# A perceiver block on one core: the order of the first loads and products, and of the last 32 microseconds

## The chip, the cores and the metric

The kernel runs on one core of a Trainium2 chip. The core has TensorE (PE, matmuls; its weight loads are the rows PEld), VectorE (DVE), ScalarE (ACT), GpSimd (POOL) and SyncE (SP, which here only issues DMAs), each with an instruction stream of its own; they wait for each other on semaphores. The metric is device time of one execution in microseconds, as the median of several runs; a lower time is better. TensorE's clock has two levels, 1.2 and 2.4 GHz; a profile gives the granted share (0.50 or 1.00).

## What is computed

Three residual layers over x, 8 x 64 tokens of 1024 numbers, all in float32, cut here to what matters:

```python
x = x + xattn(layernorm(x), ctx_4096, ...)     # cross attention, 32 heads of 128, 8 kv heads
x = x + attn(layernorm(x), Wq, Wk, Wv, Wo)     # causal self attention, 32 heads of 32
x = x + ffn(layernorm(x), W_res, W_pre, W_post, bases, gate, W_branch)

def ffn(x):                                     # 4 streams of 256 for each token
    x_norm = x * rsqrt(mean(x * x) + eps)
    logits = x_norm @ [W_res; W_pre; W_post].T + base          # 24 numbers a token
    H_res  = sinkhorn_log(logits[:16].reshape(4, 4))           # 50 iterations of row and column sums
    H_pre, H_post = softmax(logits[16:20]), softmax(logits[20:24])
    H_res  = (1 - g) * I + g * H_res
    y      = einsum('nc,n->c', streams, H_pre) @ W_branch
    return einsum('ij,jc->ic', H_res, streams) + outer(H_post, y)
```

## The kernel before

The 512 tokens are four tiles of 128 rows, t = 0 to 3; `xr[:, t, :]` is tile t of x in SBUF. A weight is used in units of 512 x 1024: a unit is loaded into `raw`, transposed there by DVE in four pieces (`turn_first`, `turn_unit`; two of the eight column chunks a piece), and split into a high part (`hi_w`, ACT, semaphore `w_hi`) and a low part (`lo_unit`, a subtraction on DVE, semaphore `w_lo`). Activations are split in the same way (`hi_ln` on ACT, `ln_lo_half` on DVE). A product takes three matmuls for each of 8 chunks c: p = 0 is high times high, p = 1 uses the low part of the weights, p = 2 the low part of the activations. The order on every engine is the order of the code; there is no scheduler.

**The start.** SP and ACT issue the loads of x and of unit 0. Unit 0 comes in two halves of 1 MB (`first_unit(0)`, `first_unit(1)`, four DMAs of 256 KB each, two from SP and two from ACT). The code numbers chunks so that a half of the columns gives chunks 0 to 3 and the other chunks 4 to 7. DVE takes the statistics of a tile (`first_stats`), POOL its power of -0.5 (`ln_root`, `ln_move`), ACT normalises into `hb`, PE transposes it (`turn_ln`), and ACT and DVE split the result. PE starts the products of unit 0 (`products`, from `query_unit(0, ...)`), for tile 0 by chunks: `chunks=True` makes it wait for `w_lo` of each chunk. The transposes of the next tile are put between the products of the present one (`between`, at the product `at`, 11 if nothing is given).

**The end.** The last 16 groups of 24 products are b = 0 to 15 (`tile_products`, with hooks `at_5`, `at_11`, `at_17` after products 5, 11 and 17). Around them PE transposes finished tiles (`turn_rows`) and multiplies them by the 24 columns of the ffn's logits (`logits`, 8 small matmuls a tile). Group b = 15 gives the last half of tile 3; DVE adds it (`add_last(3, 1)`), PE transposes it and finishes the logits of tile 3, and only then can the second of two Sinkhorn chains start on DVE. Chain 0 holds tiles 0 and 1, chain 1 tiles 2 and 3; each operation of a chain is on 128 x 32 or 128 x 8 numbers and waits for the one before it (`stepped`, semaphores `sk_step`). Chain 0 is 12 iterations ahead (`LEAD`); the rest of its iterations alternate operation by operation with those of chain 1, and the last 11 iterations of chain 1 run alone. When a chain is done, ACT writes 16 diagonal matrices a tile (`diagonals`) and PE uses each for a matmul of 256 columns (`mix`); ACT copies the result (`mixed`) and SP stores it. Tile 3 is mixed on DVE instead. In the wait for the chains PE does `branch` and `base`.

## Time and profile before

| | |
|---|---|
| median of 3 runs | 1115.98 us (1114.47 to 1116.58) |
| profiled execution, its own time | 1116.33 us |
| profiled execution, span of the core | 1114.5 us |
| busy in the span | PE 1066.1, PEld 895.4, DVE 815.9, ACT 479.1, POOL 190.8 us |
| moved | 111.26 MB |

The span runs from the first to the last instruction; the 1.8 us that the execution's own time has beside it lie around the program. Starts in rows below are microseconds from the start of the span.

### The profile page before, as it was taken

To read this page: it belongs to the slowest core of one execution; us is meant where nothing else is said; L and a number is where in the kernel's file an instruction comes from. 1 tells how busy PE (TensorE), PEld (TensorE's weight loads), DVE (VectorE), ACT (ScalarE), POOL (GpSimd) and SP (SyncE) were. 2 spreads that over 40 slices of the span, in tenths; PEclk is the share of its full clock that TensorE was granted. 3 is DMA by queue.
4 is the path that set the end of the run, shared out by engine and by line. 5 is a ranking of instruction groups with operands and counts; after the bars stand their busy time and mean duration, and the time that the engine had idled before them with its cause. 6 is when DMAs were issued, how large, how long until landed. Compare 5 with 4: busy or idle time off the path is not lost.

```text
span 1114.5 us, 17571 instructions
## 1 busy us (share of the span) xinstructions
PE 1066.1 (96%) x6326; PEld 895.4 (80%) x6326; DVE 815.9 (73%) x1854; ACT 479.1 (43%) x1021; POOL 190.8 (17%) x186
## 2 busy tenths in 40 slices
PE   5999999999999999999999999999999999999638
PEld 3888888788888888888888888888888878887537
DVE  6787667676667879766668877666627788847997
ACT  4553444344445446544444465423213344431416
POOL 0000000233233232333233230000001032320000
PEclk9999999999999999999999999999999999998779
DMA  9785676245544333344444312799935423000001
GB/s 238 153 201 129 156 158 158 50 109 109 113 96 88 75 76 72 68 96 98 109 98 108 76 38 52 159 219 244 204 67 103 76 41 58 3 14 1 1 1 76
DMA packets 184540, 111.26 MB, mean 100 GB/s; under 512 B 108040, under 2 KB 174344, under 8 KB 184480
## 3 DMA queue, kind: packets, MB, share of 16 engines
q1 hardware_dynamic: 182224, 109.37, 45.3%
q10 hardware_dynamic: 2256, 1.11, 0.5%
q8 instruction: 35, 0.57, 0.2%
q14 instruction: 25, 0.20, 0.1%
HBM read 90.98 MB, written 18.94 MB: 99 GB/s over the span
## 4 chain that ended last, share of the span: by engine, by line
PE 91%; DVE 7%; DMA 1%; ACT 1%; issue 0%; ACTq 0%; POOL 0%; DVEq 0%
PE ps L608 32%; PE ps L515 15%; PE ps L575 14%; PE ps L943 9%; PE ps L501 4%; PE ps L636 4%; PE ps L619 4%; PE ps L932 2%; PE ps L719 1%; DMA raw<-in_L_xattn_q_proj_w 1%; DVE small L2057 1%; DVE small L2061 1%; DVE small L2049 1%; PE ps L852 1%; DVE small L2053 1%; DVE small L2045 1%
## 5 line engine op out<-in xcount | busy, mean ns | idle before, releaser
L608 PE MATMUL ps<-wt,act 128*128 128x512 f32 x1536 | 381.0, 394 | 0.0
L608 PEld LDWEIGHTS ps<-wt,act 128*128 128x128 f32 x1536 | 278.0, 188 | 51.8 <-issue 0.4
L515 PE MATMUL ps<-wt,act 128*128 128x512 f32 x768 | 178.0, 393 | 4.0 <-DVE wt L1513 4.0
L515 PEld LDWEIGHTS ps<-wt,act 128*128 128x128 f32 x768 | 145.2, 190 | 34.7 <-DVE act L1497 4.4
L575 PE MATMUL ps<-act,wt 128*128 128x512 f32 x672 | 153.7, 390 | 0.0
L1068 ACT ACTIVATE wt<-raw 128x512 fp32r<-128x512 f32 x192 | 106.3, 625 | 94.4 <-PE ps L515 52.6
L575 PEld LDWEIGHTS ps<-act,wt 128*128 128x128 f32 x672 | 125.8, 188 | 26.0
L1505 DVE STREAM_TRANSPOSE raw<-raw 128x1024 f32<-128x1024 f32 x92 | 107.9, 1216 | 21.4 <-DMA raw<-in_L_xattn_o_proj_w 21.4
L1513 DVE TENSOR_TENSOR wt<-raw,wt 128x512 fp32r<-128x512 f32 x176 | 109.9, 682 | 17.4 <-ACT wt L1068 17.4
L943 PE MATMUL ps<-wt,act 128*128 128x512 f32 x480 | 122.1, 402 | 0.0
L2209 POOL TENSOR_TENSOR small<-small 128x4 f32<-128x4 f32 (+2 forms) x64 | 69.0, 1080 | 257.9 <-DVE small L1527 211.5
L1170 ACT ACTIVATE G<-G,small 128x256 f32<-128x256 f32 x128 | 64.0, 502 | 102.1 <-DVE small L1641 102.0
L1497 DVE TENSOR_TENSOR act<-ps,act 128x512 fp32r<-128x512 f32 x80 | 53.9, 680 | 67.7 <-ACT act L1063 67.7
L943 PEld LDWEIGHTS ps<-wt,act 128*128 128x128 f32 x480 | 87.3, 189 | 17.6 <-POOL wt L2268 0.2
L2236 POOL TENSOR_TENSOR act<-xr,act 128x1024 fp32r<-128x1024 f32 x30 | 72.1, 2403 | 115.9 <-ACT act L1101 115.9
L1063 ACT ACTIVATE act<-ps 128x512 fp32r<-128x512 f32 x80 | 46.9, 596 | 82.8 <-PE ps L501 82.8
L501 PE MATMUL ps<-ident,G 128*128 128x128 f32 x448 | 66.9, 275 | 9.8 <-ACT G L1074 9.7
L2227 POOL TENSOR_TENSOR small<-small 128x4 f32<-128x4 f32 x32 | 12.2, 380 | 374.4 <-DVE small L1658 374.4
L501 PEld LDWEIGHTS ps<-ident,G 128*128 128x128 f32 x448 | 54.9, 141 | 22.1 <-issue 9.2
L619 PE MATMUL ps<-act 128*128 128x256 f32 x384 | 60.0, 291 | 0.6 <-issue 0.6
L1637 DVE SCALAR_TENSOR_TENSOR G<-ps,small,G 128x256 f32<-128x256 f32 x128 | 55.4, 474 | 5.1 <-PE ps L619 5.1
L636 PEld LDWEIGHTS ps<-act 128*128 128x128 f32 x384 | 54.3, 189 | 5.6 <-issue 0.4
(164 smaller groups left out, 1242.2 us busy)
## 6 DMA issues: line engine op xcount, KB each, us to landing
xr<-in_ctx SPq DMA_DIRECT2D x64, 256.0 KB, 4.8
raw<-in_L_xattn_o_proj_w SPq DMA_DIRECT2D x32, 512.0 KB, 14.1
raw<-in_L_xattn_q_proj_w SPq DMA_DIRECT2D x28, 512.0 KB, 8.9
xr<-q_rows SPq DMA_DIRECT2D x16, 512.0 KB, 4.2
ot_hi<-spare SPq DMA_DIRECT2D x64, 128.0 KB, 2.0
act<-ot_hi SPq DMA_DIRECT2D x32, 256.0 KB, 9.0
q_rows<-G SPq DMA_DIRECT2D x28, 256.0 KB, 2.6
raw<-in_L_xattn_k_proj_w SPq DMA_DIRECT2D x8, 512.0 KB, 7.2
```

What stands on the lines that cost most here:

```text
L501: tr = pe.transpose(bank[par][:, j * P:(j + 1) * P], src, ident[:])
L515: mm = pe.matmul(banks[t], lhs(p == 2, c, t), wt[:, n_slot, int(p == 1), c, :], start=(acc_from and q == 0), stop=(acc_to and q == 3 * NC ...
L575: mm = pe.matmul(acc[h], wt[:, par, int(p == 1), c, h * P:(h + 1) * P], act[:, 0, int(p == 2), c * UW:(c + 1) * UW], start=(q == 0), stop= ...
L608: mm = pe.matmul(bank, src[int(p == 2)][:, c, kt * P:(kt + 1) * P], wt[:, slot, int(p == 1), c, :], start=(q == 0), stop=(q == 3 * NC - 1))
L619: mm = pe.matmul(sacc[:, j * 256:(j + 1) * 256], lhs[p], kT[r][:, g, :], start=(p == 0 and r == 0), stop=(p == 1))
L636: mm = pe.matmul(oacc, vN[r][:, kt, g * P:(g + 1) * P], pT[p][:, kt * 256:(kt + 1) * 256], start=(n == 0), stop=(n == 5))
L943: mm = pe.matmul(acc2[t], act[:, int(n >= 23), int(p == 2), k:k + P], wt[:, n % 2, int(p == 1), c, :], start=(q == 0), stop=(q == 3 * NC - 1))
L1068: sc.activation(blocks16(wt_dst(par, 0, c)), raw_chunks(par, c) if slot is None else raw_chunks(slot, c), ACT.Copy).then_inc(w_hi, 1)
L1505: v.transpose(y, y).then_inc(w_turned, 1)
L1513: v.tensor_tensor(blocks16(wt_dst(par, 1, c)), raw_chunks(slot, c), blocks16(wt_dst(par, 0, c)).bitcast(F32), ALU.subtract).then_inc(w_lo, 1)
L2209: pool.tensor_tensor(dst, src, mhalf[:, 0:n], ALU.pow).then_inc(signals, 1)
L2236: pool.tensor_tensor(ctx_dst(ctxT, 1, kt), ctx_src(kt), ctx_dst(ctxT, 0, kt).bitcast(F32), ALU.subtract).then_inc(ctx_lo, 1)
```

## The change

- SP waits for tile 0 of x to have landed before it issues the load of tile 1, and everything behind it in its queue; ACT waits for the same before its two DMAs of the second half of unit 0.
- In unit 0, tile 0, PE no longer goes chunk by chunk: for chunks 0 to 3 first all p = 0, then p = 2, then p = 1, and then the same for chunks 4 to 7 (`by_half`). Tiles 1 to 3 take p = 2 last (`low_last`). Waits are now on `w_hi`, `hi_done`, `lo_done` and `w_lo` each where its operand is used. The transposes of tile 1 stand after product 15 instead of 11.
- The first four low parts of the weights move from DVE to POOL (`lo_first`). DVE takes the statistics of tile 1 right behind the first two transposes. ACT alternates between high parts of weights and of the activations.
- In group b = 15 the first half of tile 3's logits stands after product 5, not after product 17 behind tile 2's.
- The last 11 iterations of chain 1 are done as two interleaved chains of one tile each (names 1 and 2, 16 columns an operation).
- Before `mix(0)` PE waits until chain 0 is 30 operations from its end and does four matmuls with an identity into an unused bank. The wait ahead of `mix(1)` is gone.
- The last half of tile 2 is mixed, copied and stored in two quarters, from banks of their own.

```diff
@@ SyncE
             for dst, rows in first_unit(0)[0:2]:
                 sp.dma_start(dst, rows).then_inc(first_half, 16)
+            sp.wait_ge(x_loaded[0], 16)
             sp.dma_start(xr[:, 1, :], x_rows[:, 1, :]).then_inc(x_loaded[1], 16)
...
-            for t, half, signal, count in ((0, None, mix_out, 2), (1, None, mix_out, 4), (2, 0, mix_out, 5),
-                                           (3, 0, out_ready, 1), (3, 1, out_ready, 2), (2, 1, mix_out, 6)):
+            for t, i0, i1, signal, count in ((0, 0, 4, mix_out, 2), (1, 0, 4, mix_out, 4), (2, 0, 2, mix_out, 5),
+                                             (2, 2, 3, mix_out, 6), (3, 0, 2, out_ready, 1), (3, 2, 4, out_ready, 2),
+                                             (2, 3, 4, mix_out, 7)):
@@ TensorE
-                        c, p = divmod(q, 3)
+                        c, p = order[min(t, 1)][q] if order else divmod(q, 3)
                         if arrived and p == 0:
                             arrived(t, c)
-                        if chunks and t == 0 and p == 0:
+                        if order and p == 2 and c % 4 == 0:
+                            pe.wait_ge(lo_done, 2 * t + c // 4 + 1)
+                        if chunks and t == 0 and p == int(bool(order)):
                             pe.wait_ge(w_lo, NC * n + c + 1)
...
             def ln_ready(t, c):
+                if t == 0:
+                    pe.wait_ge(w_hi, c + 1)
                 if c % 4 == 0:
-                    pe.wait_ge(lo_done, 2 * t + c // 4 + 1)
+                    pe.wait_ge(hi_done, 2 * t + c // 4 + 1)
+            by_half = [(4 * g + j, p) for g in range(2) for p in (0, 2, 1) for j in range(4)]
+            low_last = [(c, p) for c in range(NC) for p in (0, 1)] + [(c, 2) for c in range(NC)]
-            query_unit(0, 0, lambda t: None, next_ln, chunks=True, arrived=ln_ready, at={1: 17, 2: 17})
+            query_unit(0, 0, lambda t: None, next_ln, chunks=True, arrived=ln_ready, at={0: 15, 1: 17, 2: 17},
+                       order=(by_half, low_last))
...
                     if b == 12:
                         logits(1)
+                    elif b == 15:
+                        logits(3, 0, 4)
...
                     if b == 15:
                         logits(2)
-                        logits(3, 0, 4)
...
+            pe.wait_ge(base_added, 3)
+            pe.wait_ge(sk_step[0], CHAIN_STEPS - 30)
+            for _ in range(4):
+                pe.matmul(ps[:, 6, :], ident[:], z[:, 0, 0:UW], start=True, stop=True)
             mix(0)
-            pe.wait_ge(sk_step[1], CHAIN_STEPS - 42)
             mix(1)
-            pe.wait_ge(mix_out, 1)
-            pe.matmul(mix_banks[2][1], ident[:], xr[:, 2, UW:E], start=True, stop=False)
+            pe.wait_ge(mix_out, 2)
+            for i in (2, 3):
+                pe.matmul(mix_bank(2, i), ident[:], xr[:, 2, i * CW:(i + 1) * CW], start=True, stop=False)
             mix(2)
@@ ScalarE
+            sc.wait_ge(x_loaded[0], 16)
             for dst, rows in first_unit(1)[2:4]:
                 sc.dma_start(dst, rows).then_inc(raw_loaded[0], 16)
             normalise(0)
-            hi_ln(0, 0, T)
-            for c in range(4):
-                hi_w(0, 0, c)
+            hi_w(0, 0, 0)
+            hi(0, 0, ln_dst(0, 0, 0), bank=T)
+            hi_w(0, 0, 1)
+            hi_w(0, 0, 2)
+            hi(1, 1, ln_dst(0, 0, 1), bank=T)
+            hi_w(0, 0, 3)
             normalise(1)
...
-            mixed(2, 1)
+            mixed_quarter(2)
+            mixed_quarter(3)
@@ VectorE
             turn_first(1)
+            first_stats(1)
             ln_lo_half(0, 0)
-            for c in range(4):
-                lo_unit(0, c)
-            first_stats(1)
             turn_first(2)
             turn_first(3)
             ln_lo_half(0, 1)
+            v.wait_ge(w_lo, 4)
             for c in range(4, NC):
                 lo_unit(0, c)
...
+            tiles[1:] = [(2, 1), (3, 1)]
+            ua[1:] = [uv[:, 8:12], uv[:, 12:16]]
+            ub[1:] = [uv[:, 24:28], uv[:, 28:32]]
+            iterated.append(iterated[1])
+            stepped(1)
             for _ in range(ITERS - iterated[1]):
-                iterate((1,))
-            finish_cols(1)
-            finish_gate(1)
-            finish_diagonal(1)
+                iterate((1, 2))
+            for c in (1, 2):
+                finish_cols(c)
+            for c in (1, 2):
+                finish_gate(c)
+            for c in (1, 2):
+                finish_diagonal(c)
@@ GpSimd
+            def lo_first(c):
+                pool.wait_ge(w_hi, c + 1)
+                pool.tensor_tensor(blocks16(wt_dst(0, 1, c)), raw_chunks(0, c), blocks16(wt_dst(0, 0, c)).bitcast(F32),
+                                   ALU.subtract).then_inc(w_lo, 1)
+            ln_root(0)
+            ln_move(0)
+            lo_first(0)
+            lo_first(1)
+            ln_root(1)
+            ln_move(1)
+            lo_first(2)
+            lo_first(3)
```

The first place is DVE at the start of the program. `BN_STATS` to `TENSOR_SCALAR` are a tile's statistics, `STREAM_TRANSPOSE raw` the turned weights (two rows a half), `act` rows the low part of the activations and `wt` rows the low parts of the weights. Before, from the transposes of the first half on:

```order
L1549 STREAM_TRANSPOSE raw<-raw 128x16x64 [waits first_half]
L1549 STREAM_TRANSPOSE raw<-raw 128x16x64
L1497 TENSOR_TENSOR act<-ps,act 128x4x128 [waits hi_done]
L1513 TENSOR_TENSOR wt<-raw,wt 128x512 [waits w_hi] x4
L1522 BN_STATS small<-xr 128x6 [waits x_loaded1]
L1522 BN_STATS small<-xr 128x6
L1524 BN_AGGR small<-small 128x2 [waits dv]
L1526 TENSOR_SCALAR small<-small 128x1 [waits dv]
L1527 TENSOR_SCALAR small<-small 128x1
L1549 STREAM_TRANSPOSE raw<-raw 128x16x64 [waits raw_loaded0]
```

And in the changed kernel:

```order
L1578 STREAM_TRANSPOSE raw<-raw 128x16x64 [waits first_half]
L1578 STREAM_TRANSPOSE raw<-raw 128x16x64
L1551 BN_STATS small<-xr 128x6 [waits x_loaded1]
L1551 BN_STATS small<-xr 128x6
L1553 BN_AGGR small<-small 128x2 [waits dv]
L1555 TENSOR_SCALAR small<-small 128x1 [waits dv]
L1556 TENSOR_SCALAR small<-small 128x1
L1526 TENSOR_TENSOR act<-ps,act 128x4x128 [waits hi_done]
L1578 STREAM_TRANSPOSE raw<-raw 128x16x64 [waits raw_loaded0]
L1578 STREAM_TRANSPOSE raw<-raw 128x16x64
L1526 TENSOR_TENSOR act<-ps,act 128x4x128 [waits hi_done]
L1542 TENSOR_TENSOR wt<-raw,wt 128x512 [waits w_hi,w_lo]
```

The statistics of tile 1 have moved ahead of the first `act` row, the four `wt` rows of chunks 0 to 3 are gone from DVE, and nothing but two short pieces now stands between the first transposes and the wait for the second half (`raw_loaded0`).

The second place is PE in group b = 15. `wt,act` rows are products, `ident,xr` rows transposes of a finished tile and `G,raw` rows of 128x24 logits. Before:

```order
L943 MATMUL ps<-wt,act 128x512 x24
L874 MATMUL ps<-ident,xr 128x128 x4
L943 MATMUL ps<-wt,act 128x512 x6
L883 MATMUL ps<-G,raw 128x24 x12
L943 MATMUL ps<-wt,act 128x512 x6
L874 MATMUL ps<-ident,xr 128x128 x4
L883 MATMUL ps<-G,raw 128x24 x4
```

And in the changed kernel:

```order
L958 MATMUL ps<-wt,act 128x512 x18
L899 MATMUL ps<-G,raw 128x24 x4
L958 MATMUL ps<-wt,act 128x512 x6
L890 MATMUL ps<-ident,xr 128x128 x4
L958 MATMUL ps<-wt,act 128x512 x6
L899 MATMUL ps<-G,raw 128x24 x8
L958 MATMUL ps<-wt,act 128x512 x6
L890 MATMUL ps<-ident,xr 128x128 x4
L899 MATMUL ps<-G,raw 128x24 x4
```

Of the 12 small matmuls that stood in one piece, 4 stand 12 products earlier; the last 6 products are behind the same work as before.

## Rows read from the trace of the kernel before

**Rows 1.** Page, 40 equal slices of the span: busy tenths of TensorE.

```profile
PE   5999999999999999999999999999999999999638
```

**Rows 2.** Busy time summed over the windows 43 to 500 and 500 to 984.

```profile
sum 941.00, PE 938.62 PEld 790.88 DVE 681.55 ACT 415.38 POOL 182.37; mean PE 469.31 PEld 395.44 DVE 340.78 ACT 207.69 POOL 91.19
```

**Rows 3.** Timeline of the start: start, duration, engine, instructions, [idle before, releaser].

```profile
11.46 2.37 DVE L1549 STREAM_TRANSPOSE raw<-raw 128x1024 f32<-128x1024 f32 x2 [4.65 <-DMA raw<-in_L_xattn_q_proj_w]
...
15.15 5.09 PE L515 MATMUL ps<-wt,act 128*128 128x512 f32 x12 [4.01 <-DVE wt L1513]
...
22.09 7.06 PE L515 MATMUL ps<-wt,act 128*128 128x512 f32 x30
...
43.04 7.42 PE L575 MATMUL ps<-act,wt 128*128 128x512 f32 x32
```

**Rows 4.** ACT's DMAs of the first half: issue time min/median/max, starts; then issue to landing.

```profile
L1083 ACTq DMA_DIRECT2D raw<-in_L_xattn_q_proj_w x2: 456/507/558, 1.2 to 1.7; - x2
...
DMA to landing us min/median/max: 5.2/7.5/9.8
```

**Rows 5.** SP's DMAs of the second half, the same view.

```profile
L326 SPq DMA_DIRECT2D raw<-in_L_xattn_q_proj_w x2: 547/573/599, 2.7 to 3.4; - x2
...
DMA to landing us min/median/max: 10.5/12.2/13.8
```

**Rows 6.** Window of 2 us: busy by engine, granted clock, DMA share, GB/s.

```profile
6.00:8.00 2.00, 0.00 (x0) 0.00 (x0) 0.74 (x4) 0.18 (x1) 0.75 (x2) 1.00 1.22 251
```

**Rows 7.** POOL's subtractions of weights: ns min/median/max, first and last start.

```profile
L2268 POOL TENSOR_TENSOR wt<-raw,wt x16: 1260/1294/2274, 897.6 to 982.8; 128x512 fp32r<-128x512 f32 x16
```

**Rows 8.** Timeline of group b = 15 and what follows, PE and DVE.

```profile
1020.26 2.75 PE L883 MATMUL ps<-G,raw 128*128 128x24 f32 x24
...
1022.16 0.24 DVE L1974 SCALAR_TENSOR_TENSOR G<-G,small,ps 128x24 f32<-128x24 f32 x1
...
1022.86 2.63 PE L943 MATMUL ps<-wt,act 128*128 128x512 f32 x6
...
1025.52 0.69 DVE L1803 TENSOR_TENSOR xr<-ps,xr 128x512 f32<-128x512 f32 x1 [1.58 <-PE ps L943]
...
1028.07 1.90 PE L883 MATMUL ps<-G,raw 128*128 128x24 f32 x8 [0.69 <-ACT raw L1386]
...
1030.01 0.24 DVE L1974 SCALAR_TENSOR_TENSOR G<-G,small,ps 128x24 f32<-128x24 f32 x1 [1.25 <-PE ps L883]
```

**Rows 9.** An earlier group with 16 small matmuls, timeline of PE.

```profile
997.95 1.86 PE L883 MATMUL ps<-G,raw 128*128 128x24 f32 x16
...
999.65 7.09 PE L943 MATMUL ps<-wt,act 128*128 128x512 f32 x30
```

**Rows 10.** Windows of 1 us, as in rows 6; the granted clock is third from the end.

```profile
1023.00:1024.00 1.00, 1.00 (x4) 0.77 (x4) 0.80 (x4) 0.00 (x0) 0.00 (x0) 0.60 0.00 0
...
1091.00:1092.00 1.00, 1.00 (x5) 0.81 (x4) 0.83 (x5) 1.00 (x5) 0.00 (x0) 0.77 0.00 0
```

**Rows 11.** Two chains interleaved: one operation of two successive iterations, timeline of DVE.

```profile
1074.74 0.31 DVE L2041 TENSOR_TENSOR small<-small 128x32 f32<-128x32 f32 x2
...
1076.12 0.31 DVE L2041 TENSOR_TENSOR small<-small 128x32 f32<-128x32 f32 x2
```

**Rows 12.** Chain 1 alone, window 1087.4 to 1102.6: busy us, mean ns, idle before.

```profile
L2061 DVE RECIPROCAL small<-small 128x8 f32<-128x8 f32 x11 | 2.2, 203 | 0.4
```

**Rows 13.** The same operation on one column, elsewhere in the kernel.

```profile
L2125 DVE RECIPROCAL small<-small 128x1 f32<-128x1 f32 x1 | 0.2, 163 | 0.0
```

**Rows 14.** The end: what the chain that ended last holds, start, us.

```profile
1087.05 16.26 PE ps L932 x64
...
1103.83 0.40 ACT raw L1459
1104.27 7.19 PE ps L932 x32
```

**Rows 15.** Timeline of DVE: the last operation of chain 1.

```profile
1103.16 0.23 DVE L2116 TENSOR_SCALAR small<-small 128x8 f32<-128x8 f32 x1
```

More of the change, by code:

```diff
@@ L214, in perceiver @@
             "ones_ready", "s24_done", "s24_ready", "h8_in", "h8_out", "gate_exp"))
[L215 removed]
+        sk_step, sk_in, sk_out = ([sem(f"{n}{c}") for c in range(3)] for n in ("sk_step", "sk_in", "sk_out"))
         d_mix, base_done, base_added, h_ready, d_res, mix_done, mix_out = (sem(n) for n in (
@@ L531, in _, with query_unit @@
             pe.wait_ge(ident_ready, 16)
-            def query_unit(n, par, before=None, between=None, chunks=False, arrived=None, at=None):
+            def query_unit(n, par, before=None, between=None, chunks=False, arrived=None, at=None,
+                           order=None):
                 if not chunks:
@@ L925, in mix @@
             def mix(t):
-                for half in range(2):
-                    bank = mix_banks[t][half]
-                    for i in (2 * half, 2 * half + 1):
-                        for j in range(NSTR):
-                            pe.wait_ge(d_res, 16 * t + 4 * i + j + 1)
-                            mm = pe.matmul(bank[:, (i % 2) * CW:(i % 2 + 1) * CW], dres[t % 2][:, 4 * i + j, :],
-                                           z[:, t, j * CW:(j + 1) * CW], start=False, stop=(i % 2 == 1 and j == NSTR - 1))
-                    mm.then_inc(mix_done, 1)
+                for i in range(NSTR):
+                    for j in range(NSTR):
+                        pe.wait_ge(d_res, 16 * t + 4 * i + j + 1)
+                        mm = pe.matmul(mix_bank(t, i), dres[t % 2][:, 4 * i + j, :], z[:, t, j * CW:(j + 1) * CW],
+                                       start=False, stop=j == NSTR - 1 and (i % 2 == 1 or (t, i) == (2, 2)))
+                    if i % 2 == 1 or (t, i) == (2, 2):
+                        mm.then_inc(mix_done, 1)
             def tile_products(n, t, at_11, at_17, at_5=None):
@@ L1991, in answered, with of @@
                 v.wait_ge(sk_out[c], count)
-            def of(y, c, n=32):
-                return y[:, n * c:n * c + n]
+            tiles = [(0, 2), (2, 2)]
+            def of(y, c, n=16):
+                t, nt = tiles[c]
+                return y[:, n * t:n * (t + nt)]
             def rows3(y):
@@ L2218, in ln_move @@
                 pool.tensor_tensor(lnb[:, t:t + 1], lnm[:, t:t + 1], lnr[:, t:t + 1], ALU.mult).then_inc(ln_shift, 1)
-            for k in range(NT):
+            def lo_first(c):
[10 more added lines that the diff above has]
+            lo_first(3)
+            for k in (2, 3):
                 ln_root(k)
```

37 lines of the change are left out of this document (21 added, 16 removed).

## The prediction

> **What bounds the kernel now.** The page's slices come first: PE is at 9 tenths in all of them but the first and the last three [rows 1]. The windows of the middle say it exactly: of the 941 us from 43 to 984, PE is busy 938.6 [rows 2]. So in the middle nothing but PE's work counts, and it starts when unit 0 is done: a microsecond by which PE reaches that point earlier is a microsecond at the end, as long as the loads behind it keep up. That leaves two places, and the change is only in these.
>
> At the start [rows 3] PE's first 12 products begin at 15.15 and take 5.09 us, 0.42 each; the next 30, from 22.09, take 7.06, 0.235 each. The first are at the slow level of the clock. What they wait for is a chain: DVE waits 4.65 us for the first half of unit 0, turns it from 11.46, ACT and DVE split it. The last DMA of that half was issued by ACT at about 1.7 and took 9.8 us, so it landed at 11.5 [rows 4]. From 22.09 PE runs without a stop to 43.04 with 84 products of unit 0 left, and unit 1 follows.
>
> At the end the chain runs through group b = 15, the logits of tile 3 and the second Sinkhorn chain. DVE is through with its other work and waits 1.58 us for PE before it adds the last half of tile 3 at 1025.52; the logits of tile 3 are read at 1030.01, again after a wait for PE [rows 8]. From there DVE is the bound until chain 1's last operation ends at 1103.39 [rows 15]. ACT starts tile 2's diagonals 0.44 later, at 1103.83, because it is still copying what `mix(1)` left at 1103.3, and PE's last 32 rows take 7.19 us to 1111.46 [rows 14].
>
> **The start, part by part.** The last piece of the second half, issued by SP at 3.3, took 13.8 us: it landed at 17.2 [rows 5]. Before the change nobody felt that, because DVE came to it only at 18.4. Now DVE has little left between the halves, so I work from both landings, F for the first half and S for the second.
>
> F: through the second half, 3.2 MB have to move (0.06 identity, 0.52 for each of two tiles of x, 1.05 for each half). Without tile 1 and the second half, 1.64 MB are ahead of F; at the 251 GB/s of [rows 6], and with about 0.84 MB moved by the landing of tile 0 at 5.05, F would be 8.3. Bounds are 8.3 and the old 11.5. I take 9.5. DVE then turns until F + 2.4 = 11.9, has tile 1's statistics (1.8 us) and the low activations (0.65) by 14.4. POOL's low parts cost 1.29 us each by the median, 2.27 at worst [rows 7], with tile 1's root and shift (0.8) between the second and the third: started at F + 1.9, the fourth is done at about 17.5. PE's four p = 1 products of the first half follow; it has done the eight others in the wait. So chunks 0 to 3 are behind PE at about 18, whatever F is within a microsecond or so.
>
> S now decides. After S come two transposes (2.4), ACT's last high part and PE's product of chunk 7 (1.3 together), the 8 transposes of tile 1 (1.3), then 8 products (1.9): tile 0 is done at S + 6.9. Before it was done at 22.09 + 12 x 0.235 = 24.9. With S at 17.2 the start gains 0.8; with 3.2 MB moved at 251 GB/s and nothing in between, S is 13.9 and it gains 4.1. The second half is now issued 3 us later, but so are tiles 2 and 3 and unit 1 behind it. I take 16.0: gain 2.0. Against this stands the clock. PE's products now come singly over some nine microseconds, and a stretch with few products can leave the clock at its slow level: in [rows 10] it fell at 1023.3 behind 24 rows of small matmuls. If tile 0's last 8 products and the 9 behind them were slow, that would cost 17 x 0.19 = 3.2 us at the most; I take 0.5. **Start: 1.5 us gained** (bounds -2.4 to 4.1). Later work is covered: POOL is idle there, and unit 1, which DVE turned at 31.45, had landed by 28.1.
>
> One rule of the skill speaks against the first edit. SP's load of tile 1 stood behind its two loads of the first half in one queue anyway; what could delay the first half was the traffic of another kind, and ACT's last piece landed together with tile 1, at 11.4 and 11.5. The Trainium skill, "DMA: Bandwidth & Descriptors", section "Queues, rings and completion order", says that a DMA engine consumes the descriptors of one ring in order and takes turns between rings. By that rule the wait takes nothing from in front of SP's pieces, and F stays nearer 11.5 than 8.3. The sum above is little changed by it: with F at 11.5, POOL's fourth is done at 19.6, tile 0 at 23.8 to 24.3, and the start still gains about 0.9.
>
> **Group b = 15.** 24 rows of small matmuls take 2.60 us up to the next products, 0.108 each [rows 8]. Behind them the clock fell, at 1023.3 [rows 10], and the last 6 products took 2.63 us. Behind 16 such rows it stayed up: 30 products took 7.09, 0.236 each [rows 9]. So the last 6 should take 1.4 to 1.6 and end 1.0 us earlier. But DVE cannot use all of it. Tile 2's logits, which it read at 1022.16 without waiting, are now complete only at 1022.9 to 1023.0, since 8 rows moved ahead of them; DVE's work from there to the add was 1.78 us, so the add is at 1024.8, 0.7 earlier, and DVE, not PE, is what is late next. If the clock stays up, the 4 transposes and 8 rows behind the add take 1.5 us less as well (the 8 rows took 1.90 and would take 0.93), and then DVE's own 3.24 us from the add to the end of the iteration decide: 1028.05 against 1030.01, 1.9 earlier. The gain is 0.7 with the clock down and 1.9 with it up; I take 1.5. A bound of 0 would be a fall of the clock in the same place.
>
> **Chain 1 in two.** Two interleaved chains take 1.38 us an iteration [rows 11]; one alone takes 15.2 / 11 = 1.38 too, from the same window as [rows 12]. So an iteration costs the latency of its six operations, and a second chain is free. With 16 columns instead of 32 each operation is shorter. A reciprocal takes 203 ns on 8 numbers and 163 on one [rows 12, 13]: 4 fewer save 23 ns. If all six saved that, 11 iterations would save 1.5 us; if the 0.23 from one operation to the next did not depend on size at all, nothing. I take 1.0, and 0.1 back for the second chain's last operations.
>
> The Trainium skill, "VectorE: DVE Perf Modes", section "TRN2 errata — SBUF-src ops pay a fixed extra latency per instruction", gives a fixed term of some 150 cycles and one cycle a number at 0.96 GHz. As an estimate from that page, four operations save 16 cycles and two save 4, which is 0.83 us over 11 iterations. The trace agrees as to its kind, with 40 ns for 7 numbers of a reciprocal even more than the page gives.
>
> **Warm-up and order at the end.** After base 3 PE is idle 14 us; `mix(0)` starts slow, and the clock rises at 1091.5 [rows 10]. Its 32 rows took 9.35 us and those of `mix(1)` 6.9, 16.26 together [rows 14]. The four new matmuls start 30 operations (6.9 us) before chain 0's end, at 1078.9, and take 4 x 1.71 = 6.8 us at the slow level (twice the 0.86 of such a matmul before `mix`), so they end before 1087.05 and delay nothing. With the clock up, `mix(0)` takes 6.9 too: PE is done at 1100.9 and ACT at 1101.5, before tile 2's matrices are asked for. That is worth the 0.4 us of ACT's delay, and without it the gain of the divided chain would be lost behind ACT, for `mix(1)` would still end at 1103.3. The wait that is gone was long met, PE being in `mix(0)` until 1096.4. The last copy is of 256 columns instead of 512 and its store half as large: 0.2 to 0.5, I take 0.3. **Sum: 1.5 + 1.5 + 1.0 - 0.1 + 0.4 + 0.3 = 4.6 us.** The profiled execution took 1116.33, so 1111.7. The median of 1115.98 is 0.35 below it and the lowest run 1.9 below; if those had the clock up in b = 15, their gain is smaller, and the two cancel.
>
> **The rivals.** A change of less than 0.2% (2.2 us) is about what a measurement of this kernel cannot tell from none; faster therefore means below 1113.8.
> 1. *The forecast*, 1111.7: 0.52. Its own range is 1110.2 to 1113.2.
> 2. *The second half is as late as before and the clock is down behind it*: the start gives 0 or a little less, the end its 3.1. For it: 17.2 in [rows 5] had no effect before and has now. Against it: less traffic stands beside it. 1116.3 - 3.0 = 1113.3: 0.22.
> 3. *Both halves come early*, S near 14: the start gives 3.8. 1116.3 - 6.9 = 1109.4: 0.12.
> 4. *The clock stays low at the end*: small matmuls in two pieces still let it fall, or the idle stretch behind the warm-up does. The end gives 0.7, the start 1.5. 1114.1: 0.11. The Trainium skill, "TensorE: Matmul & The Clock Gate", section "Why this matters for your kernels", warns that an idle gap between bursts of matmuls drops the clock; by that rule the gap behind the warm-up could undo it.
> 5. *Slower*: the held-back transfers. DVE stands in front of S and everything behind it is late one for one. To be slower by 2.2 us with the end's 3.1 gained, the start must lose 5.3, so S must be 24.9 + 5.3 - 6.9 = 23.3. Bytes speak against it: at 251 GB/s that is 5.4 MB, more than all of x and unit 0. 1118.5: 0.03.
>
> **How the numbers follow.** The time is rival 1's. Leaving out half of the early case and the slow one, and the last third of the fourth, gives 1109.3 to 1114.2. Faster: 0.52 + 0.12, 0.15 of the second's 0.22 and 0.04 of the fourth's 0.11, 0.83 in all. Same: the rest of these, 0.14. Slower: 0.03.
>
> **What would show it.** The first row of DVE's transposes (F) before 10; its third transpose with a wait for `raw` that ends at 15 to 17 (S); unit 1's products at 40.5 to 42.5 instead of 43.04. In b = 15 a granted clock of 1.00 up to the last products and an add behind DVE's own work, not behind a wait for PE. In the last 11 iterations a step of 1.27 to 1.31 us instead of 1.38. `mix(0)` and `mix(1)` in about 14 us with the clock at 1.00, and ACT's diagonals of tile 2 right behind the chain. I am wrong if S is past 18, if a step stays at 1.38, or if the clock falls in the gap between warm-up and `mix(0)`.

## The result and the profile after

| | before | after |
|---|---|---|
| median of 6 runs | 1115.84 us (1113.58 to 1116.58) | 1110.12 us (1109.02 to 1110.64) |
| profiled execution, its own time | 1116.33 us | 1110.10 us |
| span | 1114.5 us | 1108.3 us |

The ratio is 0.9950, with a 95% interval of 0.9939 to 0.9961: 5.6 us faster, where 4.6 were forecast. The two profiled executions are 6.2 us apart. The rows below say where. The 5.6 are probably on the high side: four of the six runs before took over 1115.6 us, while of 69 runs of the same kernel beside the experiments 23 did, and three kernels that keep the whole change and differ from it in one wait or one order (e7, e8, e10) have ratios of 0.9954 to 0.9958, 4.7 to 5.1 us.

The start, first DVE and then PE of the changed kernel in order of time (starts in us):

```profile
9.34 2.37 DVE L1578 STREAM_TRANSPOSE raw<-raw 128x1024 f32<-128x1024 f32 x2 [2.59 <-DMA raw<-in_L_xattn_q_proj_w]
11.64 1.25 DVE L1551 BATCH_NORM_STATS2 small<-xr 128x6 f32<-128x512 f32 x2
...
15.10 2.37 DVE L1578 STREAM_TRANSPOSE raw<-raw 128x1024 f32<-128x1024 f32 x2 [1.12 <-DMA raw<-in_L_xattn_q_proj_w]
```

```profile
13.83 2.92 PE L524 MATMUL ps<-wt,act 128*128 128x512 f32 x8 [0.21 <-ACT wt L1088]
17.15 2.06 PE L524 MATMUL ps<-wt,act 128*128 128x512 f32 x5 [0.40 <-POOL wt L2261]
19.04 1.04 PE L508 MATMUL ps<-ident,G 128*128 128x128 f32 x8
19.84 6.17 PE L524 MATMUL ps<-wt,act 128*128 128x512 f32 x26
...
39.90 5.38 PE L591 MATMUL ps<-act,wt 128*128 128x512 f32 x23
```

F, the first half, is at 9.34 (11.46 before [rows 3]) and S, the second, at 15.10 (18.41 before). From 19.84 a product takes 0.237, so the clock is not slow behind the products that came singly. Tile 0 is done 8 products later, at 21.7, which is S + 6.6. Unit 1 starts at 39.90 instead of 43.04: 3.14 us gained.

That lead stays at 3.1 to 3.4 us up to 970. There DVE's subtraction meets POOL's low parts of unit 24, and PE waits. First the subtraction in the kernel before, then rows of DVE, POOL and PE in the changed one:

```profile
973.06 1.23 DVE L1882 TENSOR_TENSOR raw<-raw,small 128x1024 f32<-128x1024 f32 x1
```

```profile
969.78 2.35 DVE L1909 TENSOR_TENSOR raw<-raw,small 128x1024 f32<-128x1024 f32 x1
```

```profile
966.04 5.01 POOL L2320 TENSOR_TENSOR wt<-raw,wt 128x512 fp32r<-128x512 f32 x4 [3.51 <-ACT wt L1088]
```

```profile
975.04 0.65 PE L853 MATMUL ps<-ident,raw 128*128 128x128 f32 x4 [1.10 <-DVE act L1930]
```

Before, the subtraction took 1.23 us and POOL's four took 6.01. Now DVE's is 1.1 longer, DVE's next low part is late and PE waits 1.10 for it: about 1.0 us of the lead is gone.

Group b = 15, PE and then DVE:

```profile
1020.73 1.63 PE L958 MATMUL ps<-wt,act 128*128 128x512 f32 x6
1023.32 0.66 PE L890 MATMUL ps<-ident,xr 128*128 128x128 f32 x4 [0.95 <-DVE xr L1830]
1024.66 1.07 PE L899 MATMUL ps<-G,raw 128*128 128x24 f32 x8 [0.69 <-ACT raw L1410]
```

```profile
1020.93 0.24 DVE L2001 SCALAR_TENSOR_TENSOR G<-G,small,ps 128x24 f32<-128x24 f32 x1 [0.99 <-PE ps L899]
...
1022.62 0.64 DVE L1830 TENSOR_TENSOR xr<-ps,xr 128x512 f32<-128x512 f32 x1
...
1025.77 0.24 DVE L2001 SCALAR_TENSOR_TENSOR G<-G,small,ps 128x24 f32<-128x24 f32 x1
```

The last 6 products take 1.63 us and the last 8 rows 1.07, at the full clock [rows 8]. Tile 3's logits are read at 1025.77 instead of 1030.01: 4.24 ahead, 2.1 of it gained in this group. The end, DVE (chain 0's last operation, one operation of two successive iterations of the divided chain, the last operation of tiles 2 and 3), then PE and ACT:

```profile
1082.12 0.23 DVE L2147 TENSOR_SCALAR small<-small 128x8 f32<-128x8 f32 x1
...
1083.27 0.26 DVE L2072 TENSOR_TENSOR small<-small 128x16 f32<-128x16 f32 x2
...
1084.53 0.26 DVE L2072 TENSOR_TENSOR small<-small 128x16 f32<-128x16 f32 x2
...
1097.65 0.36 DVE L2147 TENSOR_SCALAR small<-small 128x4 f32<-128x4 f32 x2
```

```profile
1074.78 6.54 PE L1048 MATMUL ps<-G,ident 128*128 128x512 f32 x8 [5.81 <-DVE small L2092]
1082.84 14.08 PE L946 MATMUL ps<-G,raw 128*128 128x256 f32 x64 [1.52 <-ACT raw L1483]
```

```profile
1097.91 4.79 ACT L1483 ACTIVATE raw<-ident,small 128x128 f32<-128x128 f32 x16 [0.36 <-DVE small L2147]
...
1105.58 0.38 ACT L1492 ACTIVATE xr<-ps 128x256 f32<-128x256 f32 x1 [1.34 <-PE ps L946]
```

From chain 0's last operation to tile 2's, DVE needs 15.53 us (from 1082.12); before it was 16.83, from 1086.33 to 1103.16 [rows 15]: 1.30 gained by the division. `mix(0)` and `mix(1)` take 14.08 instead of 16.26 [rows 14], ACT starts tile 2's diagonals 0.26 behind the start of the chain's last operation instead of 0.67 (0.4), and copy and store are 0.3 shorter. Sum: 3.1 - 1.0 + 2.1 + 1.3 + 0.4 + 0.3 = 6.2.

### The profile page after: what moved, and what is told of

Same layout as the page of the kernel before. It is cut to its first block, busy times and chain, and to the rows that moved or that the text cites. A ratio compares the mean times of both kernels' runs of the same rounds, so it can differ in the third digit from the quotient of the medians.

```text
span 1108.3 us, 17664 instructions
## 1 busy us (share of the span) xinstructions
PE 1068.6 (96%) x6336; PEld 894.6 (81%) x6336; DVE 815.5 (74%) x1919; ACT 479.4 (43%) x1022; POOL 194.8 (18%) x190
## 4 chain that ended last, share of the span: by engine, by line
PE 88%; DVE 9%; DMA 1%; ACT 1%; issue 0%; SPq 0%; DVEq 0%
PE ps L624 32%; PE ps L524 15%; PE ps L591 14%; PE ps L958 9%; PE ps L508 4%; PE ps L652 4%; PE ps L635 4%; PE ps L735 1%; DVE small L2088 1%; DVE small L2080 1%; DVE small L2092 1%; DVE small L2084 1%; DVE small L2076 1%; DVE small L2072 1%; DMA raw<-in_L_xattn_q_proj_w 1%; PE ps L868 1%
## 5 line engine op out<-in xcount | busy, mean ns | idle before, releaser
L1534 DVE STREAM_TRANSPOSE raw<-raw 128x1024 f32<-128x1024 f32 x92 | 107.9, 1216 | 21.7 <-DMA raw<-in_L_xattn_o_proj_w 21.7
L1542 DVE TENSOR_TENSOR wt<-raw,wt 128x512 fp32r<-128x512 f32 x172 | 107.4, 682 | 17.3 <-ACT wt L1088 17.2
## 6 DMA issues: line engine op xcount, KB each, us to landing
raw<-in_L_xattn_o_proj_w SPq DMA_DIRECT2D x32, 512.0 KB, 14.1
```

What stands on the lines that cost most here:

```text
L1534: v.transpose(y, y).then_inc(w_turned, 1)
L1542: v.tensor_tensor(blocks16(wt_dst(par, 1, c)), raw_chunks(slot, c), blocks16(wt_dst(par, 0, c)).bitcast(F32), ALU.subtract).then_inc(w_lo, 1)
```

## The experiments

Twelve kernels ran in four groups, each on one chip with runs of the kernel before beside it; the changed kernel was not run again with them. The ratio is to the kernel before on the same chip; 0.001 is 1.1 us. The columns behind it are of one profiled execution each. x0 is DVE's start on tile 0 of x, 0.02 to 0.03 us behind its landing, F and S as above, U1 the first product of unit 1. "Sub" is DVE's subtraction at about 970, "fall" the moment in b = 15 at which the granted clock drops (worked out from its share in slices of 1 us), "late" the time from the start of the chain's last operation on tile 2 to ACT's first diagonal of tile 2, "mix" the time of `mix(0)` and `mix(1)`. "b15" is the reading of tile 3's logits. "Fall" and "b15" are counted from U1, with 1.1 taken off where the subtraction was long; by the starts of the small rows of b = 15 this puts the same work beside each other to within 0.7 us with the new order of the logits and 0.2 with the old one.

| kernel | ratio (interval) | x0 | F | S | U1 | sub | fall | b15 | mix | late |
|---|---|---|---|---|---|---|---|---|---|---|
| before | 1 | 5.03 | 11.46 | 18.41 | 43.04 | 1.23 | 980.2 | 987.0 | 16.2 | 0.67 |
| changed | 0.9950 (0.9939-0.9961) | 4.97 | 9.34 | 15.10 | 39.90 | 2.35 | 984.9 | 984.8 | 14.1 | 0.26 |
| e1 start only | 0.9984 (0.9973-0.9995) | 5.47 | 10.05 | 16.33 | 41.16 | 2.32 | 986.4 | 984.6 | 17.1 | 1.47 |
| e2 no hold | 0.9963 (0.9951-0.9975) | 5.10 | 11.45 | 17.79 | 42.61 | 1.23 | 983.8 | 985.6 | 14.1 | 0.26 |
| e3 logits only | 0.9995 (0.9986-1.0004) | 5.32 | 11.18 | 18.13 | 42.79 | 1.23 | 984.8 | 984.9 | 16.2 | 0.56 |
| e4 division only | 0.9998 (0.9989-1.0006) | 5.15 | 11.08 | 18.04 | 42.70 | 2.36 | 980.7 | 986.8 | 16.5 | 2.22 |
| e5 no warm-up | 0.9964 (0.9950-0.9977) | 5.09 | 9.55 | 15.65 | 40.46 | 1.23 | 985.2 | 984.7 | 16.5 | 2.22 |
| e6 lows on DVE | 0.9967 (0.9955-0.9979) | 4.85 | 9.35 | 16.30 | 41.10 | 1.23 | 986.3 | 984.9 | 14.1 | 0.26 |
| e7 lo_out2 first | 0.9954 (0.9940-0.9967) | 5.11 | 9.59 | 15.76 | 40.55 | 1.24 | 984.0 | 984.8 | 15.8 | 1.51 |
| e8 POOL waits | 0.9958 (0.9945-0.9972) | 5.05 | 9.31 | 15.10 | 39.88 | 1.23 | 984.0 | 985.8 | 14.1 | 0.26 |
| e9 SP's wait alone | 0.9965 (0.9953-0.9976) | 4.89 | 9.46 | 16.16 | 41.43 | 1.23 | 985.4 | 984.7 | 14.1 | 0.26 |
| e10 second hold | 0.9957 (0.9942-0.9971) | 4.84 | 9.27 | 15.19 | 40.01 | 2.35 | 987.0 | 984.7 | 14.1 | 0.25 |
| e11 end only | 0.9979 (0.9970-0.9988) | 4.85 | 11.40 | 18.36 | 43.02 | 2.33 | 985.2 | 985.2 | 14.1 | 0.26 |
| e12 gated warm-up | 0.9964 (0.9950-0.9977) | 6.23 | 10.95 | 17.70 | 42.50 | 1.23 | 984.8 | 985.0 | 14.1 | 0.27 |

Side by side on one chip ran e1 to e4, e5 to e8, and e9 to e11; e12 ran in a group of its own.

**e1: the changes of the start alone.**

> The kernel before with the changes of the start alone (both waits for tile 0, by_half and low_last, lo_first on POOL, the new orders of ACT and DVE). Theory A, each part acts by itself: unit 1's products start at 39.9 as in the changed kernel (43.04 before), 3.1 us. Of this the middle gives back about 1.0 near 970, where in the changed kernel a subtraction of DVE (128x1024) took 2.35 us instead of 1.23 beside POOL's low parts of unit 24. Total 2.1 us faster than before, 3.1 if that meeting does not happen here. Theory B, the start's gain is not real at the end because some later load or wait gives it back: total under 1 us.

1113.4 us against 1115.09, 1.8 us faster by the ratio: near theory A's 2.1 (the sum of its parts), but the interval goes from 0.6 to 3.0 us and doesn't quite shut out "under 1 us". U1 gained 1.9 here, not 3.1, because tile 0 landed 0.44 later and S came at 16.33; and 1.1 went at 970. At the end the kernel lost 0.8 more behind ACT ("late" 1.47 for 0.67), with `mix` at 17.1 us. One row mattered beyond the start; PE in group b = 15, with the old order of the logits:

```profile
1019.43 2.75 PE L893 MATMUL ps<-G,raw 128*128 128x24 f32 x24
1022.03 1.61 PE L953 MATMUL ps<-wt,act 128*128 128x512 f32 x6
...
1025.77 1.07 PE L893 MATMUL ps<-G,raw 128*128 128x24 f32 x8 [0.69 <-ACT raw L1400]
```

The 24 rows stand together and the clock stays up behind them.

**e2: without the two waits.** One line is taken out of SP's code and one out of ACT's:

```diff
-            sp.wait_ge(x_loaded[0], 16)
-            sc.wait_ge(x_loaded[0], 16)
```

> The changed kernel without the two waits for tile 0 of x (SP ahead of the load of tile 1, ACT ahead of its second-half DMAs). Theory A, the held transfers made both halves early: the first transposes go back from 9.3 to 11.5 and the third to 17.2 or so, tile 0 is done at 17.2 + 6.6 = 23.8 instead of 21.7, and the kernel is 2.1 us slower than the changed one, 3.6 faster than before. Theory B, the new order of products, low parts and activations made the gain, and the waits only change which bytes come first: first transposes at 9.3, no difference in time.

F is back at 11.45, S at 17.79, and U1 is 2.7 later than in the changed kernel, as theory A says. The profiled executions are 2.5 us apart: 2.7, less the 1.1 of its short subtraction, and 0.8 more in b = 15. The ratios are 0.0013 (1.4 us) apart, with overlapping intervals. Which piece was late is shown by the landings of the first half, SP's line and ACT's, in this kernel:

```profile
L328 SPq DMA_DIRECT2D raw<-in_L_xattn_q_proj_w x2: 421/450/480, 1.2 to 1.7; - x2
DMA to landing us min/median/max: 6.3/6.9/7.5
...
L1102 ACTq DMA_DIRECT2D raw<-in_L_xattn_q_proj_w x2: 455/507/559, 1.2 to 1.7; - x2
...
DMA to landing us min/median/max: 5.4/7.6/9.8
```

and in the changed one:

```profile
L328 SPq DMA_DIRECT2D raw<-in_L_xattn_q_proj_w x2: 421/450/480, 1.2 to 1.7; - x2
DMA to landing us min/median/max: 6.1/6.6/7.2
...
L1103 ACTq DMA_DIRECT2D raw<-in_L_xattn_q_proj_w x2: 460/510/559, 1.2 to 1.7; - x2
...
DMA to landing us min/median/max: 5.2/6.4/7.6
```

SP's pieces hardly move (7.5 to 7.2). ACT's last piece does, from 9.8 to 7.6. What was beside it is the traffic in SP's queue that the wait now holds back, tile 1 first of all, which in e2 landed together with it.

S is less clear. It moved by 2.7 us too, and here a transfer from behind in the same queue may have a part. SP's pieces of the second half and then its loads of tiles 2 and 3, in e2:

```profile
L331 SPq DMA_DIRECT2D raw<-in_L_xattn_q_proj_w x2: 653/668/682, 2.7 to 3.4; - x2
...
DMA to landing us min/median/max: 10.6/12.5/14.3
...
L333 SPq DMA_DIRECT2D xr<-in_x x2: 1132/1184/1235, 4.1 to 5.3; - x2
...
DMA to landing us min/median/max: 12.4/12.6/12.8
```

The last piece, issued at 3.4, landed at 17.8; tile 2, issued behind it at 4.1, landed at 16.5 to 16.9, ahead of it. In the changed kernel the last piece lands at 15.1 and tile 2 at 16.2. How much of S's 2.7 us is due to which held transfer was not separated.

**e9 and e10: which hold, and one more.** e9 takes out ACT's wait alone. e10 adds a wait in SP's queue behind the second half:

```diff
+            sp.wait_ge(first_half, 64)
             for t in (2, 3):
                 sp.dma_start(xr[:, t, :], x_rows[:, t, :]).then_inc(x_loaded[t], 16)
```

> The changed kernel with SP's wait for tile 0 kept and ACT's wait taken out, so that only tile 1, SP's two pieces of the second half and what is behind them in SP's queue are held. In the profiles so far unit 1's products start 24.8 us after the third transpose (S) in every kernel with the new order: with both waits S is 15.1 to 16.3, with neither 17.8. Theory A, what delays the first half is traffic of any queue: ACT's 0.5 MB go beside it again, F is about 10 and S about 16, half of the way. Theory B, SP's wait does it all: F 9.3, S 15.1, unit 1 at 39.9, no difference to the changed kernel. Theory C, ACT's wait does it all: F 11.5, S 17.8, 2.7 us later.

> The changed kernel with one more wait in SP's queue: tiles 2 and 3 of x and unit 1 are issued only when the first half of unit 0 has landed. Theory A, the traffic behind the second half delays it, as tile 1 did with the first: S comes 0.6 to 1.6 earlier, at 13.5 to 14.5, and unit 1's products 24.8 after it; 0.6 to 1.6 us faster than the changed kernel. Theory B, tiles 2 and 3 stand behind the second half in the same queue and take nothing from it: no difference. Against both: if tile 2 or unit 1 is then late, DVE waits for it at 20 or at 28 and the kernel is slower.

e9: F is 9.46, so SP's wait alone makes the first half early, as theory B said, and S is 16.16, as theory A said. U1 is S + 25.3, not 24.8, and none of the three theories named why. With ACT's 0.5 MB beside it, tile 1 took 8.6 us to land instead of 6.2, and its statistics on DVE came late:

```profile
13.48 1.29 DVE L1550 BATCH_NORM_STATS2 small<-xr 128x6 f32<-128x512 f32 x2 [1.65 <-DMA xr<-in_x]
...
16.16 2.37 DVE L1577 STREAM_TRANSPOSE raw<-raw 128x1024 f32<-128x1024 f32 x2 [0.30 <-DMA raw<-in_L_xattn_q_proj_w]
```

They stand ahead of the low activations, for which PE then waited 1.17 us at 15.91. ACT's wait is worth 1.5 us of U1 in these profiles. In time e9 is 0.7 us behind e10, which keeps the wait, by the medians on the same chip; the intervals overlap.

e10: tiles 2 and 3 were issued at 9.3 instead of 6.4 and unit 1 at 10.1 instead of 7.4, and S is 15.19 for 15.10. That is theory B: once the waits for tile 0 are there, holding back what stands behind the second half in its own queue brings nothing. The ratio, 0.9957, doesn't differ from the changed kernel's. The Trainium skill, "DMA: Bandwidth & Descriptors", section "Queues, rings and completion order", says that a DMA engine works through one ring in order and takes turns between rings. By that rule tile 1 could delay ACT's piece of the first half but not SP's, and the trace agrees, with 9.8 to 7.6 and 7.5 to 7.2.

**e6: the first low parts on DVE again.** Four `lo_unit` behind `ln_lo_half(0, 0)`, and none of `lo_first`.

> The changed kernel with the first four low parts of the weights back on DVE, right behind the first low activations (2.48 us for four on DVE, 1.26 each on POOL). Theory A: DVE comes to the second half at 16.4 instead of 15.1, where it had waited 1.1 us for the transfer, and tile 0 is done 1.3 us later: 1.3 us slower than the changed kernel. Theory B: PE's own products bound that stretch (it also waited 0.4 us for POOL's fourth low part), so DVE's delay costs 0.5 or less.

F is the same (9.35); DVE comes to the second half without a wait, at 16.30, and U1 is at 41.10, 1.2 later. That is theory A, as far as the profile tells. In time it is 0.0009 behind e8, which ran on the same chip, inside the intervals. In all eight profiles with the new order of products and both waits (this one is among them), and in e2, U1 is S + 24.8 within 0.03.

**e7 and e8: the meeting of DVE and POOL.** e7 moves `lo_out2` of group 9 ahead of the two transposes; e8 lets POOL wait:

```diff
+            pool.wait_ge(s2_ready, 8)
             for c in range(NC):
                 lo_unit(24, c)
```

> The changed kernel; in group b = 9 DVE does the low part of the attention output (lo_out2) ahead of the last two transposes of unit 24 instead of behind them. Theory A, the start's missing 1.1 us went into PE's wait of 1.10 us at 975.0 for that low part: the wait is gone and the kernel is 1.1 us faster than the changed one, whether or not the subtraction of DVE still takes 2.35 us. Theory B, the wait only moves to what comes behind (the transposes of unit 24, its low parts, the add of tile 1 or 2): no difference.

> The changed kernel; POOL waits for DVE's subtraction of group b = 9 (s2_ready at 8) before it begins the low parts of unit 24. Theory A, the two hold each other up because both work at once: DVE's subtraction takes 1.23 us instead of 2.35, POOL ends its eight low parts later but without cost, PE's wait at 975.0 is gone, 1.1 us faster than the changed kernel. Theory B, the 2.35 us have another cause than POOL's work beside it: the subtraction stays at 2.35, or POOL's delay of 5 us reaches the products of unit 24: no gain or slower.

DVE's and POOL's rows of e8:

```profile
969.74 1.23 DVE L1909 TENSOR_TENSOR raw<-raw,small 128x1024 f32<-128x1024 f32 x1
```

```profile
971.04 10.00 POOL L2320 TENSOR_TENSOR wt<-raw,wt 128x512 fp32r<-128x512 f32 x8 [8.45 <-DVE raw L1909]
```

Apart, both are fast: 1.23 us, and 1.25 for each of POOL's eight, 10.00 in all. The wait of PE is gone. In the 12 profiles without this wait one of the two always pays, and never both: where the subtraction takes 2.3 POOL's first four take 5.0 (five kernels), where it takes 1.23 they take 6.0 (seven, before among them). Starts decide it, narrowly: in the five POOL's fourth begins 0.01 to 0.05 us ahead of the subtraction, in the seven the subtraction begins 0.07 to 0.11 ahead. It is not the earlier start of the program that tips it: e4 and e11 begin as the kernel before does and have the long subtraction, e5, e6 and e7 begin as the changed kernel does and have the short one. What goes with it in all 12 is a row of PE just ahead, the 64 small matmuls whose result DVE takes next: 1.14 us in the seven, 1.27 to 1.31 in the five. Why these take longer in some executions is open. POOL's four, before and then after (ns min/median/max, first and last start):

```profile
L2268 POOL TENSOR_TENSOR wt<-raw,wt x4: 1260/1293/2274, 969.4 to 973.2; 128x512 fp32r<-128x512 f32 x4
```

```profile
L2320 POOL TENSOR_TENSOR wt<-raw,wt x4: 1270/1294/1302, 966.0 to 969.8; 128x512 fp32r<-128x512 f32 x4
```

Before, DVE began at 973.06, ahead of POOL's fourth at 973.17, which took 2274 ns. After, POOL's fourth begins at 969.75 and takes its usual time, and DVE's begins at 969.78 and takes 2.35 us. The Trainium skill, "SBUF — State Buffer", section "SBUF: two separate sides", describes an exclusive lock between a DVE operation with two inputs in SBUF and a GpSimd operation that reads SBUF. By that rule the first holds the ports and the other waits it out, and the rows agree: the later one is longer by 1.1 us (DVE) and 1.0 us (POOL), and 1.27 and 1.12 us of the other were left.

But neither version is measurably faster (0.9954 and 0.9958 against 0.9950). In e7's profile the meeting, which comes ahead of what e7 moves, fell the other way by itself, so that e7 didn't test its order. In e8 the clock fell at 984.0, which cost 0.8 in b = 15. That either edit brings 1.1 us in time was not shown.

**e3: the logits alone.**

> The kernel before with only the first half of tile 3's logits moved to product 5 of group b = 15. Theory A, the clock: with 16 rows of small matmuls in one piece instead of 24 it stays at 1.00 to the end of the group, the last 6 products take 1.63 instead of 2.63 us, and tile 3's logits are read 2.1 us earlier; 2.1 us faster than before. Theory B, only the order counts: DVE's add of tile 3 is held by tile 2's logits, 0.7 us faster. If the clock falls at the same place all the same: 0.

1114.81 against 1115.09: the interval of the ratio holds 1 and reaches to 1.6 us faster, so theory A's 2.1 is refuted as a gain of the median. Its profile shows theory A's picture, the last 6 products at the full clock and the logits read at 984.9. But e1, with the old order, has them at 984.6: its clock stayed up behind the 24 rows. With the old order the clock fell at 980.2 (before), 980.7 (e4) and 986.4 (e1); with the new one between 983.8 and 987.0, in eleven profiles. An early fall costs 2.0 to 2.3 us: from the first of the 24 small rows to the reading it is 9.7 us in the kernel before and 9.4 in e4, 7.4 in e1. With the new order a fall at 984, on the last 8 small rows, costs 0.3 (e7) to 0.8 (e2, e8), and a later one nothing.

How often the early fall comes is told by the runs, each of which has its mean granted clock. The profiles of before and e4, with the early fall, have 0.983, e1's has 0.988 and e3's 0.986. Of 69 runs of the kernel before beside the experiments, 17 have 0.983; they took 1115.6 to 1117.9 us, median 1117.1. The other 52 have a median of 1114.6, and 6 of them are over 1115.6. None of the 11 runs of e3 has 0.983, and none took over 1115.9. So the move takes away a cost of about 2.5 us that the kernel before pays in about one execution of four. On average that is 0.6 us, and 0.5 was measured. The mean of a run doesn't say where its clock was low, so the link rests on these profiles.

**e4 and e5: division and warm-up, each without the other.** e5 takes out

```diff
-            pe.wait_ge(base_added, 3)
-            pe.wait_ge(sk_step[0], CHAIN_STEPS - 30)
-            for _ in range(4):
-                pe.matmul(ps[:, 6, :], ident[:], z[:, 0, 0:UW], start=True, stop=True)
```

> The kernel before with only the last 11 iterations of chain 1 divided in two; no warm-up, the last half of tile 2 mixed and copied as before. Theory A: the chain ends 1.3 us earlier (iterations of 1.27 instead of 1.38), but mix(1) still ends at 1103.3 at the place of before, ACT copies it until 1103.8, and tile 2's diagonals cannot start sooner than they did: 0 to 0.1 us faster. Theory B, the divided chain brings its whole 1.3 us by itself.

> The changed kernel without the four warm-up matmuls and the two waits ahead of them. Theory A: mix(0) starts with the clock at 0.50, mix(0) and mix(1) take 16.3 us instead of 14.1, mix(1) ends at 1099.1 and ACT's last copy of it about 1099.6, so tile 2's diagonals start 1.7 us later than the 1097.9 of the changed kernel: 1.7 us slower than the changed kernel, 4.0 faster than before. Theory B, ACT and mix(1) have slack behind the chain: no difference.

e4, DVE's last operation of tile 2 and ACT:

```profile
1102.58 0.36 DVE L2120 TENSOR_SCALAR small<-small 128x4 f32<-128x4 f32 x2
```

```profile
1104.31 0.60 ACT L1464 ACTIVATE xr<-ps 128x512 f32<-128x512 f32 x1 [2.86 <-PE ps L932]
1104.80 1.56 ACT L1459 ACTIVATE raw<-ident,small 128x128 f32<-128x128 f32 x5
```

The division gives its 1.30 on DVE (15.54 from chain to chain) and all of it is lost: ACT copies `mix(1)` until 1104.8 and starts the diagonals 2.22 behind the chain. The ratio is 0.9998, theory A. e5 has the same 2.22, with `mix` at 16.5: 1.96 us later than the changed kernel at the place itself, where theory A said 1.7. By the medians it is 1.2 us behind e8, which ran on the same chip; the intervals overlap.

**e11: the end alone.**

> The kernel before with all the changes of the end (logits, divided chain, warm-up, quarters) and none of the start. Alone, the logits gave 0.5 us and the divided chain 0. Theory A, the parts of the end need each other: the divided chain's 1.3 us reach the end only if mix(0) and mix(1) take 14.1 us instead of 16.2, so that with the 0.4 of ACT's delay, 0.3 of the quarters and the logits' 0.5 on the average it is 2.5 us faster than before, up to 4.4 where the clock falls early in the kernel before. Theory B, parts add up: 0.5 + 0 + 0.3, about 1 us faster.

2.3 us faster (1.3 to 3.3), which is theory A; e3 and e4 gave 0.8 together by their ratios, both within noise of nothing. Start alone 1.8 and end alone 2.3 make 4.1 of the 5.6. The rest is no more than the intervals allow; 0.8 of it would fit e1, whose slow `mix` held back in its profile what the warm-up frees.

**e12: a warm-up without a gap.** In e7 the clock rose at 1079.1 and fell again at 1082.5, right as `mix(0)` began (windows of 1 us; the granted clock is third from the end):

```profile
1079.00:1080.00 1.00, 1.00 (x3) 0.25 (x2) 1.00 (x11) 0.00 (x0) 0.00 (x0) 0.94 0.00 0
1081.00:1082.00 1.00, 0.00 (x0) 0.00 (x0) 0.98 (x8) 0.09 (x1) 0.00 (x0) 1.00 0.00 0
1082.00:1083.00 1.00, 0.63 (x2) 0.54 (x3) 0.81 (x5) 1.00 (x4) 0.00 (x0) 0.77 0.00 0
1083.00:1084.00 1.00, 1.00 (x4) 0.81 (x3) 1.00 (x11) 1.00 (x5) 0.00 (x0) 0.50 0.02 8
```

PE had been idle for 2 us. e12 has e8's wait and this:

```diff
-            for _ in range(4):
+            for _ in range(3):
                 pe.matmul(ps[:, 6, :], ident[:], z[:, 0, 0:UW], start=True, stop=True)
+            for left in (14, 11, 8, 5, 2):
+                pe.wait_ge(sk_step[0], CHAIN_STEPS - left)
+                pe.matmul(ps[:, 6, 0:CW], ident[:], z[:, 0, 0:CW], start=True, stop=True)
```

> The changed kernel with POOL waiting for DVE's subtraction (s2_ready at 8) as before, and another warm-up: three matmuls of 512 columns from 30 operations before the end of chain 0, then five of 256 columns, released 14, 11, 8, 5 and 2 operations before it, so that PE is not idle between the warm-up and mix(0). In one profile so far the clock fell again in that gap and mix(0) with mix(1) took 15.8 us, in six it took 14.1. Theory A: the clock is at 1.00 from about 1081 to the end, mix(0) and mix(1) take 14.1, tile 2's diagonals start 0.3 after the chain, the subtraction takes 1.23, and the runs' middle value is 0.3 to 0.6 us below the changed kernel's ratio of 0.9950 to before (0.9945 to 0.9947). Theory B: released by DVE's steps, the small matmuls come late or slow and push mix(0) back by 0.3 us or more: ratio 0.9953 or above.

```profile
1076.58 5.44 PE L1048 MATMUL ps<-G,ident 128*128 128x512 f32 x6 [6.19 <-DVE small L2095]
1081.83 2.35 PE L1051 MATMUL ps<-G,ident 128*128 128x256 f32 x10
1084.64 14.08 PE L946 MATMUL ps<-G,raw 128*128 128x256 f32 x64 [0.46 <-ACT raw L1486]
```

At its place it does what theory A says: `mix` 14.1, "late" 0.27, nothing pushed back. In time theory A's 0.9945 to 0.9947 did not come: the ratio is 0.9964, and its interval (0.9950 to 0.9977) begins above them. In the profiled execution, the slowest of its five, the reason is one that neither theory had: tile 0 of x came at 6.23, and with the holds all of the start came later, U1 at 42.50. Whether the other four ran so is not known. From U1 to the last copy e12 takes 1064.9; the others that begin as the changed kernel does and have `mix` at 14.1 take 1064.6 to 1065.7. No version was found that beats the changed kernel.

## Why the prediction was right, and where its sum was not

- **F and S.** 9.5 forecast, 9.34 measured; 16.0 forecast, 15.10 measured; tile 0 at S + 6.9, measured S + 6.6; 0.5 us set aside for a slow clock, not needed. Together they turn the 1.5 of the start into 3.1. The mechanism holds (e2, e6), S is the mis-sized term. That S decides whatever F is was right (S + 24.8 with F from 9.3 to 11.5). That POOL's parts are off the path was right too: PE waits 0.40 for one, but U1 is S + 24.8 with them on DVE as well (e6).
- **The rule on the queues** was read correctly and applied to the wrong pieces. "By that rule [...] F stays nearer 11.5": the text itself said that ACT's last piece was the late one, and for pieces of another queue the rule says the contrary. F came at 9.34.
- **A term was missing.** The sum assumed that the start's lead reaches the end. 1.0 us of it went near 970 in the profiled execution, where DVE began 0.03 us behind POOL and waited for it. [rows 7] had the other side of it, the 2274 ns of one of POOL's.
- **Group b = 15.** 1.5 forecast, 2.1 in the pair of profiles, and the picture was as described: clock at 1.00, an add behind DVE's own work, 0.7 earlier. "So the last 6 should take 1.4 to 1.6" held in all eleven profiles of the new order (1.63). What failed is that the sum takes the early fall of [rows 10] for the kernel's habit. By the granted clock it came in 17 of 69 runs; alone the move gave 0.5 us, not told from nothing. The text saw this for the lowest runs and no further.
- **Chain 1 in two.** 1.0 less 0.1 forecast, 1.30 measured, with iterations of 1.26 us. The interplay was right: without the warm-up it is worth nothing (e4).
- **Warm-up, ACT, quarters.** 0.4 and 0.3 forecast and measured; 14.1 us for the two mixes forecast as "about 14". Rival 4's gap is real: it struck in e7, and there cost 1.25 us behind the chain.
- **The sum.** 4.6 forecast against 6.2 in the profiled pair and 5.6 by the ratio; the time 1110.12 lies in the range, just below the forecast's own 1110.2, towards rival 3, whose early S is half of what happened. That it came so near is partly luck: the start was 1.6 too small and the missing term 1.0 the other way, and the kernel before happened to be profiled with the early fall of the clock, without which b = 15 is not worth 2.1. By their times most of its six runs had it too.

## What to carry to other kernels

Here the first half came early by holding back what was issued beside it in *another* queue; a further hold on what stood behind the second half in its own queue changed nothing (e10), and a hold on a landing makes the whole start as late as that landing. A shortened chain pays only if the engine behind it is ready sooner too: look at what that engine is doing at the new end. And a single profile shows one phase: where a cost hangs on which of two engines starts first, or on where the clock falls, look at several executions before giving an edit the credit. The mean granted clock of each run, set beside its time, costs nothing and tells two kinds of executions apart here.

## What the runs showed that was not expected

- At about 970 one of DVE and POOL waits out nearly the whole operation of the other: 2.35 us for 1.23, or 6.01 for 5.01, decided by about a tenth of a microsecond in their starts.
- One execution in four of the kernel before is about 2.5 us longer than the others, and its mean granted clock is 0.983.
- The clock's fall in b = 15 wanders over 3.2 us (new order) or 6.2 us (old order) against the same work, and one idle stretch of 2 us behind the warm-up let the clock fall (e7), where 1.5 (changed) and 2.5 us (e2, e6, e8) did not.
- The first 0.5 MB load reached DVE between 4.84 and 6.23 us in 14 profiles (in 13 of them by 5.47), though nothing ahead of it differs.
